# Odd tokens projected and evicted first, batch 0's pair sums on VectorE, weight preparation partly on ScalarE

## The reference, cut to what matters

```python
xn = layernorm(x)
q, k, v = heads(xn @ Wq.T + bq), heads(xn @ Wk.T + bk), heads(xn @ Wv.T + bv)
q, k = exp(q), exp(k)
kv = cumsum(k[:, :, :, None] * v[:, :, None, :], axis=1)   # over the 256 tokens
k1 = cumsum(k, axis=1)
att = (q @ kv) / sum(q * k1)
x1 = x + layernorm(att @ Wo.T + bo)
t = rms_norm(layernorm(x1)) * gamma_x;  se = rms_norm(slot_embeds) * gamma_slot
logits = t @ se.T                                          # 256 tokens x 512 slots
slots = softmax(logits, over the tokens).T @ t
processed = gelu(slots @ w1) @ w2
out = x1 + layernorm(softmax(logits, over the slots) @ processed)
```

## Time and profile before

| what | us |
|---|---|
| median of 3 runs | 641.02 (640.26 to 642.71) |
| the profiled execution's own time | 639.47 |
| its span, first to last instruction | 637.6 |
| PE busy (matmuls) | 584.0, 92% |
| POOL busy | 488.8, 77% |
| DVE busy | 478.1, 75% |
| ACT busy | 444.8, 70% |

### The profile page before, as it was taken

The page is one execution under the profiler, slowest core; times in us unless marked ns, Lnnn a source line. Parts: engine busy times, 40 slices in busy tenths (PEclk is TensorE's granted clock), DMA queues, the critical chain, the costliest instruction groups (busy, mean ns, idle before and its releaser), DMA issues.

```text
span 637.6 us, 11570 instructions
## 1 busy us (share of the span) xinstructions
PE 584.0 (92%) x4136; PEld 516.0 (81%) x4136; DVE 478.1 (75%) x929; ACT 444.8 (70%) x1065; POOL 488.8 (77%) x501
## 2 busy tenths in 40 slices
PE   2346999999999999999999999999999999999886
PEld 1235788989888888989888888989888888988775
DVE  7877778777778878777778778777778788767621
ACT  3234777777777777777777777777777777777765
POOL 4997788888888888888888888888888888874100
PEclk9955999999999999999999999999999999999999
DMA  3000000000000000000000000000000000000000
GB/s 107 8 17 9 18 9 17 26 26 26 26 21 22 18 17 26 27 26 26 27 19 24 17 19 26 26 26 26 26 18 25 17 18 26 18 27 9 9 9 16
DMA packets 16828, 14.34 MB, mean 22 GB/s; under 512 B 2850, under 2 KB 16644, under 8 KB 16772
## 3 DMA queue, kind: packets, MB, share of 16 engines
q1 hardware_dynamic: 14708, 12.76, 6.8%
q10 hardware_dynamic: 2064, 0.86, 0.5%
HBM read 5.25 MB, written 4.19 MB: 15 GB/s over the span
## 4 chain that ended last, share of the span: by engine, by line
PE 63%; DVE 25%; ACT 5%; issue 3%; POOL 2%; DMA 1%; SPq 0%; DVEq 0%; POOLq 0%; ACTq 0%
PE HB L675 16%; DVE WB L883 13%; PE LA L656 9%; PE LA L688 8%; PE LA L635 5%; PE WB L607 3%; PE WB L533 3%; PE HB L664 2%; PE WB L608 2%; DVE att L893 2%; PE WB L558 2%; PE LB L645 2%; DVE xnT_lo L856 2%; PE WB L591 2%; ACT xnT_hi L394 2%
## 5 line engine op out<-in xcount | busy, mean ns | idle before, releaser
L675 PE MATMUL HB<-w_c,hid 128*128 128x128 f32 x1024 | 124.6, 275 | 0.7 <-ACT hid L398 0.7
L675 PEld LDWEIGHTS HB<-w_c,hid 128*128 128x128 f32 x1024 | 121.0, 192 | 1.1 <-ACT hid L398 1.1
L306 POOL TENSOR_TENSOR kv<-E 128x1024 f32<-128x1024 f32 x32 | 68.5, 2140 | 38.3 <-ACT E L394 38.2
L398 ACT ACTIVATE hid<-HB 128x512 f32<-128x512 f32 x128 | 76.5, 597 | 25.3 <-PE HB L535 22.0
L868 DVE TENSOR_TENSOR prod<-WB,E 128x768 f32<-128x768 f32 x96 | 90.5, 943 | 4.6 <-PE WB L608 4.5
L313 POOL TENSOR_TENSOR kv_lo<-kv,kv_hi 128x1152 fp32r<-128x1152 f32 x32 | 85.2, 2661 | 0.0
L883 DVE TENSOR_REDUCE WB<-prod 128x288 f32<-128x2304 f32 x32 | 82.0, 2561 | 3.2
L361 POOL TENSOR_TENSOR kv<-kv,kv_prev 128x1024 f32<-128x1024 f32 x32 | 76.6, 2393 | 0.0
L306 POOL TENSOR_TENSOR kv_prev<-prev 128x1024 f32<-128x1024 f32 x32 | 68.3, 2134 | 0.5 <-DMA prev<-E 0.4
L656 PE MATMUL LA<-xn,disp 128*128 128x129 f32 x512 | 62.5, 275 | 0.8 <-ACT disp L394 0.8
L688 PE MATMUL LA<-proc,comb 128*128 128x129 f32 x512 | 62.5, 274 | 0.7 <-ACT proc L394 0.7
(11 more groups left out here) (134 smaller groups left out, 1519.6 us busy)
## 6 DMA issues: line engine op xcount, KB each, us to landing
X<-in_L_attn_x_dram SPq DMA_DIRECT2D x32, 128.0 KB, 2.1
out_dram<-res SPq DMA_DIRECT2D x32, 128.0 KB, 1.9
prev<-E SPq DMA_DIRECT2D x32, 112.0 KB, 2.1
w_in<-in_L_ffn_w_dram ACTq DMA_DIRECT2D x2, 256.0 KB, 4.6
prev<-E SPq DMA_DIRECT2D x32, 15.0 KB, 2.0
se_in<-n_L_ffn_slot_embeds_dram ACTq DMA_DIRECT2D x1, 256.0 KB, 4.0
w_in<-in_L_attn_Wq_dram SPq DMA_DIRECT2D x1, 64.0 KB, 2.5
w_in<-in_L_attn_Wk_dram SPq DMA_DIRECT2D x1, 64.0 KB, 2.2
```

Source lines behind the costliest of these rows:

```text
L306: return pool.tensor_tensor(dst.rearrange("p (d h e) -> p d h e", d=HD, h=NH), k.rearrange("p (o h e) -> p o h e", o=1, h=NH).broadcast_to ...
L398: act.activation(hid[:, f, :], HB[:, f % 2, :], ACT.Gelu).then_inc(gelu_ready[f], 1)
L675: last = pe.matmul(PR[:, j, :], hid[:, f, j * P:(j + 1) * P], w2_c[:, f, :], start=(f == 0), stop=(f == FJ - 1))
```

## The change

The projection now does the odd tokens first, and the wait for `attT_ready` stands in front of both; each token's projection, Exp and v copy has its own signal. `shift_odd` waits for the odd ones, everything else for the even ones. The pair sums of batch 0 alone are made on DVE (`first_sums`), POOL leaves them out. Weight preparation: the squares and scaling of the slots, the high parts of the slots, of w1 and of the qkv weights, and the centring of w2 go to ACT; DVE keeps the low parts, each read from a PSUM bank. The norm of the slots is made on POOL with one power of -0.5, without the reciprocal and the scaling on DVE. In `step`, DVE's `wo_centre` goes behind `attention`; on POOL `slot_norms` goes to the end; on PE `wo_transpose` goes one batch later, in front of `att_transpose`, and `slot_transpose` goes behind `cumulate`.

```diff
             def project(n):
                 after(pe, xT_lo_ready, n)
                 if n == 0:
                     pe.wait_ge(s_wqkv, 1)
-                for c in range(NC):
-                    if c == 1:
-                        after(pe, attT_ready, n - 2)
+                after(pe, attT_ready, n - 2)
+
+                for c in reversed(range(NC)):
                     cols = slice(c * P, (c + 1) * P)
-                    last = three(WB[:, c, 0:QKV], xT_hi[:, cols], xT_lo[:, cols], wqkv_hi[:, :], wqkv_lo[:, :])
-                last.then_inc(qkv_done, 1)
+                    three(WB[:, c, 0:QKV], xT_hi[:, cols], xT_lo[:, cols], wqkv_hi[:, :], wqkv_lo[:, :])\
+                        .then_inc(qkv_done[c], 1)
...
             def qkv_evict(n, u):
-                after(act, qkv_done, n)
-                act.activation(E[u][:, :, 0:2 * DIM], WB[:, :, 0:2 * DIM], ACT.Exp).then_inc(qk_exp, 1)
-                copy(E[u][:, :, 2 * DIM:QKV], WB[:, :, 2 * DIM:QKV]).then_inc(v_copied, 1)
+                for c in reversed(range(NC)):
+                    after(act, qkv_done[c], n)
+                    act.activation(E[u][:, c, 0:2 * DIM], WB[:, c, 0:2 * DIM], ACT.Exp).then_inc(qk_exp[c], 1)
+                    copy(E[u][:, c, 2 * DIM:QKV], WB[:, c, 2 * DIM:QKV]).then_inc(v_copied[c], 1)
...
+            def slot_squares(n):        # ACT; DVE's own is gone
+                if n == 0:
+                    act.wait_ge(s_seload, 16)
+                    for j in range(SJ):
+                        last = act.activation(se_sq[:, j, :], se_in[:, j, :], ACT.Square, scale=1.0 / ROOT_DIM,
+                                              accum_out=se_norm[:, j:j + 1])
+                    last.then_inc(s_sesum, 1)
...
+            def w2_centre(n):
+
+                if n == 0:
+                    act.wait_ge(s_w2load, 16)
+                    for f in range(FJ):
+                        last = act.activation(w2_c[:, f, :], w2_in[:, f, :], ACT.Copy, scale=-1.0 / DIM,
+                                              accum_out=w2_mean[:, f:f + 1])
+                    last.then_inc(s_w2, 1)
+                    act.wait_ge(s_w2, 1)
+                    for f in range(FJ):
+                        last = act.activation(w2_c[:, f, :], w2_in[:, f, :], ACT.Identity, bias=w2_mean[:, f:f + 1])
+                    last.then_inc(s_w2, 1)
...
             act.wait_ge(s_const, 7)
+            act.wait_ge(s_wT, 1)
+            copy(wqkv_hi[:, :], LB[:, 0, 0:QKV]).then_inc(s_wqkvhi, 1)
             pipeline(act, step)
...
+            def first_sums(n, u):
+
+                if n == 0:
+                    loaded(dve, prev_loaded, n, 2)
+                    outer(dve, kv_prev[:, :], prev[u][:, 0:DIM], prev[u][:, DIM:2 * DIM]).then_inc(kv_odd, 1)
+                    dve.tensor_tensor(kv[:, KVF:FEAT], E[u][:, 0, DIM:2 * DIM], prev[u][:, 0:DIM], ALU.add)\
+                        .then_inc(kv_den, 1)
+                    after(dve, kv_even, n)
+                    after(dve, kv_odd, n)
+                    dve.tensor_tensor(kv[:, 0:KVF], kv[:, 0:KVF], kv_prev[:, :], ALU.add).then_inc(kv_built, 1)
+                    after(dve, kv_den, n)
+                    after(dve, kv_built, n)
+                    dve.tensor_copy(kv_hi[:, :], kv[:, :]).then_inc(kv_hi_ready, 1)
+                    after(dve, kv_hi_ready, n)
+                    low_part(kv_lo[:, :], kv[:, :], kv_hi[:, :]).then_inc(kv_lo_ready, 1)
```

More of the change, by code:

```diff
@@ L173, in attention_and_slot_mixture @@
             sem("s_" + n) for n in ("xstat", "xst", "xve", "xrs", "xneg", "xh", "xT"))
-        xT_hi_ready, xT_lo_ready, qkv_done = sem("s_xThi"), sem("s_xTlo"), sem("s_qkv")
-        qk_exp, v_copied = sem("s_qkexp"), sem("s_vcopy")
+        xT_hi_ready, xT_lo_ready = sem("s_xThi"), sem("s_xTlo")
+        qkv_done, qk_exp, v_copied = ([sem(f"s_{n}{c}") for c in range(NC)] for n in ("qkv", "qkexp", "vcopy"))
         prev_loaded = [sem(f"prev_loaded{u}") for u in range(2)]
@@ L368, in step @@
                     sums_high(t)
-                if p is not None:
-                    slot_norms(p)
-                if t is not None:
                     own_product(t, t % 2)
@@ L379, in step @@
                     x_rstd_of(q)
+                if t is not None:
+                    wo_order(t)
                 if r is not None:
                     y_rstd_of(r)
-                if t is not None:
-                    wo_order(t)
                 if p is not None:
@@ L387, in step @@
                     x1_rstd_of(r)
+                if p is not None:
+                    slot_norms(p)
             pipeline(pool, step)
@@ new lines, in slot_squares, with slot_scale @@
+            def slot_squares(n):
+                if n == 0:
+                    act.wait_ge(s_seload, 16)
[3 more added lines that the diff above has]
+                    last.then_inc(s_sesum, 1)
+            def slot_scale(n):
+                if n == 0:
+                    act.wait_ge(s_senorm, 1)
+                    for j in range(SJ):
+                        last = act.activation(se_sq[:, j, :], se_in[:, j, :], ACT.Copy, scale=se_norm[:, j:j + 1])
+                    last.then_inc(s_sescale, 1)
@@ L471, in step @@
                     x1_squares(l)
+                if t is not None:
+                    w2_centre(t)
+                if r is not None:
+                    slot_high(r)
                 if b is not None:
@@ L485, in step @@
                     gelu(b, 3)
+                if t is not None:
+                    w1_high(t)
                 if a is not None:
@@ L495, in step @@
                     y_squares(r)
+                if t is not None:
+                    slot_scale(t)
+                if p is not None:
+                    slot_squares(p)
                 if l is not None:
@@ L583, in attention_out @@
                 if n == 0:
-                    after(pe, v_copied, 2)
+                    after(pe, v_copied[0], 2)
                     after(pe, attT_ready, 0)
@@ L597, in cumulate @@
                     if n == 0:
[L598 removed]
+                        after(pe, v_copied[0], 1)
                     after(pe, kv_lo_ready, n)
@@ L702, in step @@
                     logits(l)
-                if t is not None:
-                    slot_transpose(t)
                 if r is not None:
+                    wo_transpose(r)
                     att_transpose(r)
@@ L726, in step @@
                     cumulate(t, 2)
+                    slot_transpose(t)
                 if l is not None:
                     slots_transpose(l)
-                if t is not None:
-                    wo_transpose(t)
             pipeline(pe, step)
@@ L956, in step @@
                 if r is not None:
-                    wo_centre(r)
                     own_sum(r, r % 2)
@@ L962, in step @@
                     multiply(r, r % 2, 2)
-                if p is not None:
-                    slot_squares(p)
                 if l is not None:
@@ L970, in step @@
                     xT_low(p)
+                if r is not None:
+                    wo_centre(r)
                 if t is not None:
-                    slot_scale(t)
+                    first_sums(t, t % 2)
                 if l is not None:
@@ L992, in step @@
                 if r is not None:
+                    slot_low(r)
                     first_residual(r)
+                    w1_low(r)
             pipeline(dve, step)
```

126 lines of the change are left out of this document (51 added, 75 removed).

## The result

The changed kernel takes 653.75 us (median; 653.14 to 654.42) against 640.67 for the kernel before on the same chip: a ratio of 1.0204, 95% interval 1.0184 to 1.0223. It is slower by 13.1 us. Its profiled execution took 653.16 us, with a span of 651.4. The forecast was 653.0.

The account below looks back on a forecast made before the run. One ring, PE's stretch from the attention's transposes to L614 plus 5 us of ACT and DVE, was taken to set the period. 639.47 + 15.8 (steady stalls) - 3.85 (start-up) = 651.4, plus 1.55 to the median: 653.0 us, range 647.4 to 658.9.

Parts of the forecast that it names:

- The wait in front: Steady-state projection on PE: both tokens wait for the attention's copy, 0.53 us per step, bounds 0.39 and 0.63.
- Given back behind?: Eviction on ACT behind the projection: earlier data unused, Exp waits for its table; four instructions take 0.92 against 0.76 us.
- Head: Start-up up to projection 0: one extra ACT table load, 1.28 us, cancels with DVE's lost work; within 0.2 us of before.
- Batch 1 on ScalarE: Start-up: squares and `w2_centre` precede `xT_high`, ACT free at 18.2; `xT_low` ends 1.9 us earlier.
- Batch 0's sums: Start-up, pair sums on DVE: 4.8 us, ready at 23.85 against 26.70 on POOL, 2.85 earlier; up to 1.8 at risk.
- Sum of the start: Whole start-up: `att` of batch 0 starts 3.85 us earlier, bounds 1 and 5.3.
- Total: Whole kernel: 651.4 us for the profiled execution, plus 1.55 to the median, 653.0.
- The stall was not absorbed: Denies rival 1, steady state: DVE alone sets the period and PE's `att` wait absorbs the stall; 637.2 to 638.9, chance 0.04.
- rival 2: Start-up gives nothing, as ACT's longer queue is late for batch 1: 656.8 us, chance 0.13.
- The clock did not rise a step later: Denies rival 3, start-up: added PE idle time delays the clock's rise, a whole step costing some 8 us: 661, chance 0.04.
- The change did what it says: Denies rival 4, projection: something else held the odd load, so the wait isn't effectively in front: 637 to 644, chance 0.03.
- one ring: Steady state: PE's stretch from the attention's transposes to L614, plus 5 us of ACT and DVE, sets the 17.93 us period.

Follow-up runs that it names:

- The last-but-one experiment: Changed kernel with even tokens first and the high part of the qkv weights back on DVE: 635.41 us against 640.67 for the kernel before.
- the first attempt to go below 17.95: Changed kernel with even tokens first, Gelu's table requested early and one `process` tile moved ahead of the attention's transposes: 650.86 us against 641.08 before.
- the other two: Changed kernel, even first, tile 0 moved from behind `part_transpose` to ahead of the attention's transposes: 642.86 us; also with qkv weights' high part on DVE: 640.42 us.

## Why the prediction was right, point by point

- **The wait in front.** Right, and shown from both sides: it alone makes the loss (658.33), and putting it back, or filling its hole, takes the loss away (638.03, 638.53). Predicted 0.53 per step, measured 18.51 - 17.94 = 0.57 on average and 0.59 in the step shown. The term was mis-sized by about 0.05: I let the weight load follow the copy as closely as before (0.05). It follows by 0.12 (332.10 behind 331.60 + 0.38). Over 28 steps it made 1.2 us: 16.06 for 28 x 0.53 = 14.84.
- **Given back behind?** Right: nothing. The first Exp waits for its table; the four evictions take 334.16 - 333.30 = 0.86 (I had 0.92), and with the even token first they cost nothing in the period.
- **Head.** The right parts, a wrong place. I counted one extra load (1.28) and let it cancel with what VectorE lost, so that projection 0 would be within 0.2 us; it starts at 10.96 for 9.79. The step that failed is the assumption that the first load is done before the transposes are. Before, it was, and `xT_hi` was at 7.36; after, both loads and the copy between them follow the wait. The last-but-one experiment prices the three together at 2.60 us at batch 0. The reason given for the second load (that every load follows a function that the table lacks) was wrong; it came because `step`'s request always loads. The even v was to be 0.7 earlier than before by its order; from the first matmul on it was 0.33 (13.83 - 10.96 = 2.87 us, before 12.99 - 9.79 = 3.20), so GpSimd's first product started at 13.92 and not at 12.4.
- **Batch 1 on ScalarE.** The squares were cheaper than taken (0.29 for an accumulating one, from a row of 0.39 with another operand), so ScalarE was free at 18.78 where I had 18.2, in spite of a start 1.4 later. `xh` took 0.60 for 2.52, as predicted.
- **Batch 0's sums.** 19.54 to 24.35 is 4.8 us, as predicted. They were not slowed: GpSimd waited 5.19 us for them, as the argument said.
- **Sum of the start.** Predicted -3.85 at batch 0, measured -3.47; the head took 1.2, the cheaper squares gave 0.8. Measured at batch 2 the gain is 2.32: the stalls of batches 2 and 3, which I booked separately at 0.5 each, lie in this and took 0.59 and 0.56. So -3.85 + 2 x 0.5 = -2.85 was predicted for it; the miss is 0.5.
- **Total.** Predicted +12.0 on the median, measured +13.1 (spans: +13.8). In the profiled executions the steady state was 1.2 too low and the start 0.5 too good: 13.7 measured (653.16 - 639.47) for 12.0. That miss of 1.7 shows only by 0.75 in the medians, because I added 1.55 for the distance from the profiled execution to the median, and in the changed kernel it was 0.59. The mechanism is settled; that the sum is right to 0.75 us is luck.
- **Rivals.** The stall was not absorbed (TensorE waited 14.5 us for `att`, before 14.9). The 0.47 a step that this rival had to give back is a mean that holds the start-up's long waits; in a steady step it is about 0.3. The start-up gave something (rival 2 wrong). The clock did not rise a step later (about 61 us in the profiled execution, 62.5 in that of before). The change did what it says.
- **What the prediction lacked.** It spoke of one ring. It is the right one for this edit, which lengthens TensorE's stretch, but two others lie 0.07 and about 0.3 us behind it. The second decided the first attempt to go below 17.95; that the third decided the other two is argued, not shown.

## What to carry to other kernels

A wait placed between two halves of a job, where the first half covers a copy on another engine, can be worth more than the length of that copy (here 0.57 us a step for a copy of 0.38): look at what runs on the *waiting* engine in just that time before you move it, and restore the cover with any independent work if it must be moved. When a lengthening is predicted one ring is enough, for a shortening it is not: draw every chain that leaves the same instruction, since the next one may be 0.07 us behind. When an engine with table loads takes over a small job, count where the loads then fall, not the job's own length alone (here 0.49 us of copy, and 2.60 us at batch 0).

## What the runs showed that I had not expected

- **The table load goes where the queue stands.** With the request for Gelu's table first the load ran at 5.18, while ScalarE waited for TensorE. With a copy first it came at 6.96, behind the wait, and the request's own load behind the copy, at 8.76; a request ahead of the wait moved one load to 5.18 and left the other at 7.52, as every request in `step` loads again. Each load was 1.28 us with the next instruction 0.01 to 0.02 behind it.
- **The waiting weight load follows the copy later where nothing stands between the transposes and the wait:** by 0.11 to 0.12 us in all 30 steps of the changed kernel and of both variants of the kernel before with the wait in front, by 0.04 to 0.06 in all 30 steps of the kernel before and of the variant with the even token first, where the even tokens' matmuls run up to the wait. Why is not shown.
- **The clock's rise moves between executions.** The four executions of the changed kernel fell into two pairs, 653.14 and 653.16 (granted clock 1.000), and 654.34 and 654.42 (0.992). In the profiled one the clock column reads 1.00 from the start, though 384-wide matmuls follow each other in 0.32 us in the start-up (11.44 and 11.76 below) and in 0.17 after about 61 us. Timeline of TensorE:

```profile
11.44 0.52 PE L598 MATMUL WB<-wqkv_lo,xT_hi 128*128 128x384 f32 x1
11.76 0.52 PE L599 MATMUL WB<-wqkv_hi,xT_lo 128*128 128x384 f32 x1
...
332.39 0.34 PE L598 MATMUL WB<-wqkv_lo,xT_hi 128*128 128x384 f32 x1
332.56 0.34 PE L599 MATMUL WB<-wqkv_hi,xT_lo 128*128 128x384 f32 x1
```

So the pitch of a known matmul tells the level, 1.2 or 2.4 GHz, where the column does not. The 1.2 us between the pairs is as large as some effects of the start-up; that is why the start-up is compared above by positions in the trace and not by medians alone.
